# A language-model layer in eight batches: reordered prologue, split projections, layer-norm scaling on POOL, expert weights over two steps

## The reference

```python
h = onehot(x) @ embeddings                          # 8000 x 256 table
h = h + attention(layernorm(h), w_qkv, w_proj)      # 16 heads of 16, rotary embedding, softmax over 256 keys
h = h + ffn(layernorm(h), gate_w, expert_w)
# ffn(y): chosen = argmax(y @ gate_w.T) of 8 experts; y + (expert_w[chosen] @ y)
# layernorm(h) = (h - mean) / sqrt(var + 1e-5)
```

## Time and profile before

| | us |
|---|---|
| median of 3 runs | 316.15 |
| lowest, highest | 316.15, 316.58 |
| the profiled execution | 315.12 |
| its span | 313.3 |
| mean granted TensorE clock in it | 0.998 |
| prologue, to the first `t_pair` matmul | 44.62 |

### The profile page before, as it was taken

The page is one execution under the profiler, slowest core; times in us unless marked ns, Lnnn a source line. Parts: engine busy times, 40 slices in busy tenths (PEclk is TensorE's granted clock), DMA queues, the critical chain, the costliest instruction groups (busy, mean ns, idle before and its releaser), DMA issues.

```text
span 313.3 us, 5632 instructions
## 1 busy us (share of the span) xinstructions
PE 282.4 (90%) x2073; PEld 201.9 (64%) x2073; DVE 246.3 (79%) x600; ACT 132.4 (42%) x271; POOL 86.4 (28%) x97
## 2 busy tenths in 40 slices
PE   2959988987889999989998999899999999999893
PEld 2738756555556776677766776676666666667582
DVE  8796977777997799797987798878898874566763
ACT  3155516646774533364435532463543454320100
POOL 5654005125786013431215031301210210210401
PEclk9999999999999999999999999999999999999999
DMA  3530232900940580029101840066010010000010
GB/s 115 195 129 7 74 129 58 152 9 11 146 61 9 94 115 2 2 83 146 21 0 45 143 62 4 33 110 96 2 37 3 2 36 2 4 29 5 0 36 33
DMA packets 10787, 17.55 MB, mean 56 GB/s; under 512 B 2008, under 2 KB 4867, under 8 KB 10632
## 3 DMA queue, kind: packets, MB, share of 16 engines
q1 hardware_dynamic: 9972, 16.62, 26.3%
q0 software_dynamic: 768, 0.55, 0.7%
q10 hardware_dynamic: 20, 0.02, 0.0%
HBM read 5.30 MB, written 2.10 MB: 24 GB/s over the span
## 4 chain that ended last, share of the span: by engine, by line
PE 48%; DVE 29%; issue 12%; POOL 6%; ACT 3%; DMA 1%; POOLq 0%; DVEq 0%
PE e_bank L467 14%; PE f_bank L467 7%; PE o_bank L629 7%; DVE neg_max L976 6%; DVE acc L1055 5%; PE t_pair L594 4%; POOL qk L386 3%; PE s_pair L467 2%; PE m_bank L641 2%; PE s_pair L564 2%; PE m_bank L467 2%; DVE xn L941 2%; POOL res L403 2%; DVE rope_b L963 1%; DVE rope_a L959 1%
## 5 line engine op out<-in xcount | busy, mean ns | idle before, releaser
L840 ACT ACTIVATE probs<-t_pair 128x512 f32<-128x512 f32 x128 | 69.7, 596 | 89.6 <-PE t_pair L594 89.0
L976 DVE TENSOR_REDUCE neg_max<-s_pair 128x2 f32<-128x512 f32 x128 | 82.0, 683 | 11.5 <-PE s_pair L564 11.4
L564 PE MATMUL s_pair<-stacks 48*128 48x256 f32 x256 | 48.2, 309 | 0.3 <-DVE neg_max L976 0.2
L594 PE MATMUL t_pair<-stacks 50*128 50x256 f32 x256 | 46.5, 308 | 1.6 <-DVE neg_max L976 1.1
L594 PEld LDWEIGHTS t_pair<-stacks 50*128 50x128 f32 x256 | 32.7, 185 | 23.4 <-issue 20.5
L467 PE MATMUL e_bank<-ew_h,y_h 128*128 128x512 f32 x92 | 40.3, 438 | 4.6 <-DVE acc L1051 2.7
L1055 DVE SCALAR_TENSOR_TENSOR acc<-e_bank,mask,acc 128x256 f32<-128x256 f32 x66 | 28.9, 479 | 11.2 <-PE e_bank L467 10.7
L386 POOL TENSOR_TENSOR qk<-rope_a,rope_b 128x512 f32<-128x512 f32 x16 | 20.9, 1307 | 60.4 <-DVE rope_b L963 60.4
L467 PE MATMUL e_bank<-ew_l,y_h 128*128 128x512 f32 x92 | 36.4, 395 | 0.0
L467 PE MATMUL e_bank<-ew_h,y_l 128*128 128x512 f32 x92 | 36.2, 394 | 0.0
L564 PEld LDWEIGHTS s_pair<-stacks 48*128 48x128 f32 x256 | 33.6, 185 | 3.0 <-DVE neg_max L976 1.3
(11 more groups left out here) (169 smaller groups left out, 552.9 us busy)
## 6 DMA issues: line engine op xcount, KB each, us to landing
stacks<-parts SPq DMA_DIRECT2D x36, 256.0 KB, 6.9
ew_raw<-in_expert_w SPq DMA_DIRECT2D x1, 2048.0 KB, 8.5
out<-res SPq DMA_DIRECT2D x8, 256.0 KB
stacks<-parts SPq DMA_DIRECT2D x12, 128.0 KB, 2.9
probs<-in_w_qkv SPq DMA_DIRECT2D x2, 384.0 KB, 3.5
stacks<-max_rows SPq DMA_DIRECT2D x30, 8.0 KB
h<-in_emb,ids POOLq DMA_INDIRECT x16, 5.3
probs<-in_w_proj SPq DMA_DIRECT2D x1, 256.0 KB
```

The source lines that it names most:

```text
L564: m = mm(s_pair[:, half, t * N:(t + 1) * N], stacks[b % STACKS][r:r + KS, pair, 0, t * P:(t + 1) * P], stacks[b % STACKS][r:r + KS, pair, ...
L594: m = mm(t_pair[:, half, c * N:(c + 1) * N], stacks[b % STACKS][r:r + KM, pair, 1, c * P:(c + 1) * P], stacks[b % STACKS][r:r + KM, pair, ...
L840: nc.scalar.activation(probs[:, (2 * v + half) % RING, :, :].rearrange("p c n -> p (c n)"), t_pair[:, half, :], ACT.Exp, scale=SCALE).then ...
L976: v.tensor_reduce(neg_max[:, k // 4, :, 4 * half + k % 4], s_pair[:, half, :].rearrange("p (t n) -> p t n", t=NT), AX.X, ALU.max, negate=T ...
```

## The change

Five things are changed.

1. `Z_ORDER` is the plain order: all four copies of t = 0, then those of t = 1.
2. The prologue: TensorE does `project_qk(1, 1)` between the two `z_transpose`, in the place of a fill of two matmuls; the wait for `roped` and the fill of three before the last visit are gone. DVE does `x_low(1)` before `z_low(0)`, and `f_norm_a(2)` after the first `maximum`. POOL does `gate_weights` and `proj_weights_low` after the two rotated sums of batch 0, and both of batch 1 before `f_rs_of(2)`.
3. The two projections of batch 2 are issued in halves of three matmuls, one half after each of `max_transpose(0, 0)` and the visits 5, 6 and 7.
4. From batch 2 on `xn`, and for batches 0 to 6 `yn`, is computed by POOL (`f_scale`, `g_scale`), right behind `f_rs_of` and `g_rs_of`, one slot or two before the DVE did it. New waits guard the reuse of the buffers.
5. The expert weights are taken at slots 1, 5, 9 and 13 of steps 0 and 1.

```diff
-        Z_ORDER = [(0, 0), (0, 1), (1, 0), (1, 1), (1, 2), (0, 2), (0, 3), (1, 3)]
+        Z_ORDER = [(t, q) for t in range(NT) for q in range(4)]
...
+            def f_scale(b):
+                wait(pool, f_rstd, b + 1)
+                wait(pool, xt_ps, b)
+                for t in range(NT):
+                    g.tensor_scalar(xn[:, t, :], h0[:, b * NT + t, :], f_mv[:, t, 0:1], f_rs[:, t:t + 1],
+                                    ALU.subtract, ALU.mult).then_inc(f_scaled, 1)
+
+            def g_scale(b):
+                wait(pool, g_rstd, b + 1)
+                wait(pool, yt_ps, b)
+                for t in range(NT):
+                    g.tensor_scalar(yn[:, t, :], h1[:, t, :], g_mv[:, t, 0:1], g_rs[:, t:t + 1],
+                                    ALU.subtract, ALU.mult).then_inc(g_normed, 1)
...
                     for k in batches(front, "stats", g_at):
                         f_rs_of(k)
+                        f_scale(k)
                     for k in batches(post, "stats", g_at):
                         g_rs_of(k)
+                        if not last(k):
+                            g_scale(k)
...
-                    if s % 2 and b == 1:
-                        expert_weights([s // 2])
+                    if s % 4 == 1 and b < 2:
+                        expert_weights([4 * b + s // 4])
...
             f_rs_of(1)
+            rotated_sum(0, 0)
+            rotated_sum(0, 1)
             gate_weights()
             proj_weights_low()
-            rotated_sum(0, 0)
-            rotated_sum(0, 1)
             rotated_sum(1, 0)
+            rotated_sum(1, 1)
             f_rs_of(2)
-            rotated_sum(1, 1)
+            f_scale(2)
             steps(step)
...
-                wait(pe, f_normed, b * NT + NT)
+                if b < 2:
+                    wait(pe, f_normed, b * NT + NT)
+                else:
+                    wait(pe, f_scaled, (b - 2) * NT + NT)
...
             z_transpose(0)
-            fill(s_bank[0], 2)
+            project_qk(1, 1)
             z_transpose(1)
-            project_qk(1, 1)
             visit(-1, 0)
...
-            project_qk(2, 0)
+            project_qk(2, 0, [0])
             visit(-1, 5)
-            project_qk(2, 1)
+            project_qk(2, 0, [1])
             visit(-1, 6)
-            pe.wait_ge(roped, 2 * 2 * NT)
-            fill(t_bank[0], 3)
+            project_qk(2, 1, [0])
             visit(-1, 7)
+            project_qk(2, 1, [1])
             pe.wait_ge(xl_ok, 3)
             fill(m_bank, 2)
...
             def f_norm_a(b):
                 dve.wait_ge(gathered[b], 16 * NT)
+                wait(dve, f_scaled, (b - 3) * NT + NT)
...
             def g_norm_a(b):
                 wait(dve, h1_ok, b * NT + NT)
+                wait(dve, g_normed, (b - 1) * NT + NT)
...
                     for k in batches(post, "g_norm", g_at):
-                        g_norm_b(k)
+                        if last(k):
+                            g_norm_b(k)
...
-                    for k in batches(front, "norm", g_at):
-                        f_norm_b(k)
...
             z_again(0)
+            x_low(1)
             z_low(0)
-            x_low(1)
             z_again(1)
             z_low(1)
             rotate(1, 0)
-            f_norm_a(2)
             rotate(1, 1)
             maximum(0, 0)
-            f_norm_b(2)
+            f_norm_a(2)
             maximum(0, 1)
```

More of the change, by code:

```diff
@@ L145, in tower @@
         ew_h_ok, ew_l_ok, gw_h_ok, gw_l_ok = map(sem, "ew_h_ok ew_l_ok gw_h_ok gw_l_ok".split())
-        f_stats, f_moments, f_var, f_rstd, f_normed = map(sem, "f_stats f_moments f_var f_rstd f_normed".split())
+        f_stats, f_moments, f_var, f_rstd, f_normed, f_scaled = map(
+            sem, "f_stats f_moments f_var f_rstd f_normed f_scaled".split())
         xt_ps, xh_ok, xl_ok, v_ps, v_ok, qk_ps = map(sem, "xt_ps xh_ok xl_ok v_ps v_ok qk_ps".split())
@@ L460, in _, with product @@
             tr = nc.tensor.transpose
[L462 to L468, removed]
+            def product(o, xh, xl, wh, wl, parts=range(C)):
+                for c in parts:
+                    for n, (a, w) in enumerate(((xh, wh), (xl, wh), (xh, wl))):
+                        m = mm(o, a(c), w(c), start=(c == 0 and n == 0), stop=(c == C - 1 and n == 2))
                 return m
@@ L500, in project_v, with project_qk @@
                 m.then_inc(v_ps, 1)
-            def project_qk(b, t):
-                if t == 0:
+            def project_qk(b, t, parts=range(C)):
+                if parts[0] > 0:
+                    pass
+                elif t == 0:
                     if b == 0:
@@ L515, in project_qk @@
                 x_h, x_l = x_parts(b)
-                product(front_bank(b, t)[:, :], lambda c: x_h[:, c, t, :], lambda c: x_l[:, c, t, :],
-                        lambda c: wqkv_h[:, c, 0:2 * D], lambda c: wqkv_l[:, c, 0:2 * D]).then_inc(qk_ps, 1)
+                m = product(front_bank(b, t)[:, :], lambda c: x_h[:, c, t, :], lambda c: x_l[:, c, t, :],
+                            lambda c: wqkv_h[:, c, 0:2 * D], lambda c: wqkv_l[:, c, 0:2 * D], parts)
+                if parts[-1] == C - 1:
+                    m.then_inc(qk_ps, 1)
             def qk_transpose(b, t):
@@ L895, in step @@
                         gate_row(k)
-                    if b == 1 and s % 2:
-                        expert_weights(s // 2)
+                    if b < 2 and s % 4 == 1:
+                        expert_weights(4 * b + s // 4)
             for c in range(C):
```

## The result

The changed kernel takes 325.11 us (median of 4 runs, 324.01 to 326.85), the kernel before, run beside it, 316.37 us: a ratio of 1.0277, 95% interval 1.0218 to 1.0337. It is slower by 8.7 us where 309.9 us, a gain of 6 us, was forecast; rival (c), the price of a POOL tensor_scalar, is what happened, and by more than its own figure of 321.3 us. The profiled execution took 324.01 us for a span of 322.2, 8.9 us above the span of before.

What follows compares the result with a forecast made beforehand. TensorE was taken as the bound, busy 90% of the span, with VectorE setting the prologue from 28.90. Gains of 4.0 (prologue), 1.3 (norms) and 0.9 (step 1) made 6.2 us, forecast 309.9 us, range 307.8 to 313.2.

Steps and rivals of the forecast that it cites:

- rival (c): POOL norm scalings: a tensor_scalar with two pointer operands is dear, making the kernel slower, 321.3 us at 1.28 each; chance 0.05.
- part 3: Norms moved to POOL: the expert starts 0.44 us earlier in steps 2, 3 and 4, a gain of 1.3 us.
- Rival (c)'s formula: Loss per step: T - 1.6 in 2 to 4 and 7, T - 1.1 in 5 and 6; with step 1 and prologue 8T - 11.4.
- T: Time of a pair of POOL scalings between `g_rs` and `y_transpose`; the kernel turns slower at 1.93 us, full price 2.56.
- The 4.0: Prologue to the last `maximum`: its end comes at 40.8 instead of 44.80, 4.0 us earlier; bounds 2.5 to 4.7.
- Part 1: Prologue up to the first maximum: `project_qk(1, 0)` near 20.5, `maximum(0, 0)` at 27.1, 3.0 us earlier.
- Part 2: The prologue's eight visits: 13.7 us instead of 14.7 from first to last maximum, halves costing 0.45 us over four visits.
- rival (b): Prologue visits: halves leave VectorE as much idle time as wholes; total gain 4.7, 311.4 us; chance 0.15.
- 0, and late if a scaling costs more: Prologue, `x_transpose(2)`: POOL's scaling done at 31.3, TensorE there at 31.4, so no wait.
- has two microseconds of slack and is worth 0 on both engines: Middle steps: computing the `xn` pair on POOL or on VectorE makes no difference, 0 us.
- Part 4: Expert weights spread over steps 0 and 1: `x_transpose(4)` no longer waits 0.61, step 1 gains 0.9 us, step 0 nothing.
- the clock held 1.00 through pauses of 2 us: Argument against the rival that the prologue's gain is taken back, partly by a lower clock, about 315 us; chance 0.06.

Runs made afterwards that it cites:

- norms_dve: The changed kernel with all norms of batches 2 to 7 back on VectorE, the rest of the change kept: 311.87 us, ratio 0.9824 to the kernel before.
- y_pool: `norms_dve` with `yn` of batches 0 to 6 on POOL and `xn` on VectorE: 319.56 us, ratio 1.0121 to the kernel before.
- fill_wait: The changed kernel with 12 dummy matmuls of TensorE in step 1's 3.40 us stand before `y_transpose`: 321.78 us, ratio 1.0179 to the kernel before.
- y0_on_dve: The changed kernel with `yn` of batch 0 alone (the norm in step 1) back on VectorE: 323.77 us.
- late_x_on_pool: `norms_dve` with `xn` of batches 5 to 7 (steps 2 to 4) on POOL: 310.63 us, ratio 0.9785 to the kernel before.
- weights_step1: `norms_dve` with all eight expert weight pieces in step 1, as before the change: 312.09 us, against 311.87 for `norms_dve`.
- prices: The kernel before with seven POOL instructions behind its last one, only their durations of interest: kernel's own scaling 1.23 us, tensor_tensor 0.72 us.

## Why the prediction was wrong

**The step that failed is part 3's "I take 0.45 us each, 0.9 a pair, by the one-input row".** A pair takes 2.44 us, and the gain of 1.3 us in steps 2 to 4 became a loss of 2.8. The row it was taken from is an affine_select of 128x128, 0.29 us, another function; a tensor_scalar of that size takes 0.79 us. The upper bound, a tensor_tensor of 1.28 us with twice the elements, lies next to the measured 1.23, but that is chance: a tensor_tensor of the right size takes 0.72 us, as the text had worked out (0.73), and no row of the trace before gave the price. The text had the warning itself: a pow of 128x2 takes 0.73 us, so the function sets POOL's price; it stood as a reason of rival (c) and was given 0.05.

**Rival (c)'s formula held in the steps it was made from.** With T = 2.44 it gives 0.84 for steps 2 to 4, 1.34 for 5 and 6, and 0.84 for 7. Measured against before: 1.18, 0.83, 0.76, 1.42, 1.41 and 0.70. In sum, 8T - 11.4 - 4.0 is +4.1 us, and +8.9 came. What is missing:

- *Step 1*: 0.64 by the formula, 3.79 measured. Against the 27.46 us of `norms_dve` it is 4.14, and the runs split it: 1.05 for the pair alone (`y_pool`), 1.64 more with the `xn` pair on POOL too, which with an expert weight stands ahead of `g_rs` (`fill_wait`, 30.15, less `y_pool`, 28.51), 1.45 for the clock (31.60 less 30.15). This split takes one profiled execution of each. The prediction saw that POOL's pair of batch k stands ahead of `g_rs`, and dismissed it with 2.6 us of room; the pair alone is now 2.44, and the expert weight's 1.27 behind it was not counted.
- *Steps 0 and 2*: 0.58 and 1.18 measured, 0 and 0.84 by the formula. Step 0 shows 0.75 us of waiting for POOL's `xn`; of step 2 `fill_wait` gives back 0.40 (33.80 us), so its surplus came over from step 1's long stand. Whether through the clock is open: `y0_on_dve`, which lost clock in step 1, has 33.80 in step 2 as well.
- *The prologue*: 4.0 less T - 1.0 is a gain of 2.6; the first exp is 1.77 earlier. The 4.0 was too much: with the norms on VectorE it is 2.50 (`norms_dve`), and the scaling on POOL takes 0.73 of it, where T - 1.0 is 1.44.

**Part 1 was right**: `project_qk(1, 0)` at 20.49 (near 20.5), the first maximum at 27.22 (27.1), the price of `proj_weights_low` beside VectorE about 1.0 (one copy of 1.44 instead of 0.42) where 1.1 was taken.

**Part 2 was half right.** Between its first and its last maximum VectorE of the changed kernel idles 2.10 us (0.45, 0.67, 0.29, 0.34 and 0.35), where 0.45 was taken. The halves make up 0.98 of it, three visits with 0.33 each, and whole projections 1.73: a gain of 0.75, so rival (b) was partly right. With the norms on VectorE the prologue gains 2.88 us on VectorE (44.80 to 41.92), with them on POOL 2.14: the scaling saved VectorE 0.9 us and cost `x_transpose(2)` a wait of 0.94, and idle time came in its place. The forecast said "0, and late if a scaling costs more"; it does.

**That the `xn` pair of a middle step "has two microseconds of slack and is worth 0 on both engines" was half wrong.** The slack was there; but the pair is worth 0.45 us per step on POOL (`late_x_on_pool`), and at full price; `yn` on POOL loses 0.9. The two were the wrong way round: `yn` has TensorE behind it at once, while `xn` only stood in VectorE's way.

**Part 4 (0.9 us) was not there.** With the norms on VectorE, the spread changes step 1 by 0.02 us (`weights_step1`). The spread did not clear the place beside `xn`: one of the subtractions that are left stands there too (82.34 to 83.63 in `norms_dve`), and the pair takes 0.99 us, as the 0.98 before and the 0.97 of `weights_step1`. With `xn` on POOL `x_transpose(4)` still waits, 0.58 us. What taking `xn` of step 1 from VectorE is worth by itself, no run tests.

**The clock.** That "the clock held 1.00 through pauses of 2 us" was read from one execution. The profiled executions of the changed kernel and of seven of the ten experiments have a stretch of four microseconds at 0.50 to 0.77, and the kernel before is not free of it: `prices` shows 0.76 in the prologue behind that very pause, and its runs beside `fill_wait` went from 314.83 to 318.68 us, at granted clocks of 0.978 to 0.999.

## What to carry to other kernels

A price for an engine is taken from a row of the same function; where none is in the trace, the range has to take in the dearer bound, here 1.28 us and a time above 321 us. Moving work to an engine that is three times slower at it pays only if the result has that much room: here `xn` of the middle steps had it and `yn` did not. Before work goes into a queue, read what stands behind it, whose result another engine waits for. Where TensorE must stand for microseconds, dummy matmuls are worth a try: here they left the stand's end where it was and still made the kernel 2.3 us faster by profile.

## What was not expected of the hardware

- On POOL a tensor_scalar of 128x256 takes 0.85 us (one constant) to 1.23 us (two pointers, two operations), a tensor_tensor of the same size 0.72 us. VectorE takes 0.41 us for the dearest of these forms.
- A VectorE copy beside a POOL tensor_tensor of 128x512 took 1.44 us instead of 0.42; with the POOL instruction moved, the VectorE pair beside it paid (1.78 us instead of 0.91), and the copy did not.
- After a stand of 3.40 us the next four microseconds of TensorE were granted 0.57 of full clock, and four transposes took 1.12 us instead of 0.66; with 12 dummy matmuls in the stand the clock stayed at 1.00 and the kernel was 3.3 us faster in the median.
- The same stand does not always bring the same clock: after a wait of 1.57 us at the same place TensorE was granted 1.00 in `norms_dve` and 0.81 and 0.77 in `late_x_on_pool`.
